# Two graph layers on one core: raw f32 rows gathered from x and h instead of tables of split f16 rows

## The chip, the cores and the metric

The kernel runs on 1 core of a Trainium2 chip. The metric is the device time of the whole program in microseconds. All inputs and outputs lie in HBM. The engines are TensorE (PE), VectorE (DVE), ScalarE (ACT), GpSimd (POOL) and the sequencer SyncE (SP).

## The reference

6250 nodes with 512 numbers each, 106250 edges. Edges come sorted by dst; src and dst are symmetric with one loop for each node.

```python
edge_index = jnp.stack([src, dst])
# layer 0, messages go from src to dst
x_l = x @ W_l.T + b_l
agg = segment_sum(x_l[src], dst, 6250); deg = segment_sum(ones, dst, 6250)
x = layernorm(x + agg / max(deg, 1) + x @ W_r.T)
# layer 1, h = x, messages go from dst to src
msg = h[dst] @ W_neigh.T + b_neigh
neigh = segment_sum(msg, src, n) / max(deg, 1)
y = h + relu(h @ W_self.T + b_self + neigh)
y = layernorm(y) * ln_gamma + ln_beta
out = layernorm(x + y)
```

## The kernel before, in words

Both layers first add up the raw rows of the neighbours and project the mean afterwards. The nodes stand in T = 49 tiles of 128. A layer's edges are put in a list of 928 chunks of 128 edges; two chunks (a group) belong to one tile of target nodes. For each chunk POOL gathers 128 rows with one indirect DMA (L359), VectorE makes a one-hot 128 x 128 that says which target row each edge has (L564), and TensorE multiplies one-hot by rows into one of two pairs of PSUM banks (`sums`, L764). VectorE adds a finished group to the accumulator `acc` of its tile in SBUF (`add`, L577), whose number it loads into a register. The 513th column counts the edges. The semaphore `s_mm` counts finished chunks; `add`, POOL (which reuses a row buffer) and the rings wait for it.

**Tables.** TensorE multiplies f16 in one pass. So each f32 row is stored as two f16 halves, `high` and `low`, scaled by a power of two, with the scale and its inverse in the last 4 f16 places: a table row has 1028 f16, 2056 bytes. For layer 0 the kernel loads all of x into `acc`, takes maxima (L425), and ScalarE, VectorE and POOL make the table (L837, L449, L324 to L327), which SP stores (L264) before the sort begins. For layer 1 the halves are made at the end of each tile of layer 0 (L678, L679) and stored beside `h_scratch` (L286, L288).

**Lists.** Layer 0's list is made from windows of 256 edges: loads L249 to L252, arithmetic L405 to L417, f32 matmuls (L717 to L722), copies L435 to L440. Layer 1's needs a sort by src tile: `prepare(1)` counts (L471) and finds places (L495 to L498, 49 rounds) on VectorE alone. Then each of EC = 832 columns of 128 edges is placed by a matmul of `put` (value at its row) with `where` (one-hot of the chunk, 128 x 928 in two halves). The value has two parts for f16, so there are 4 matmuls a column (`place`, L740). ScalarE makes `put1` and `put2` (L851, L852) from VectorE's `spot` (L590); VectorE makes `where` (L592). The columns are mixed into the first 832 chunks of layer 0's aggregation, one column before each chunk. The result is unpacked after layer 0's last chunk.

**Rings.** `rows` has GB = 8 buffers, `onehot` SB = 8, `put` and `where` PB = 4. The indices of 8 chunks at a time are copied by VectorE (`hand_over`, L554, L555) into a ring of 16.

**Projection.** For each tile ScalarE scales the sums to means (L865), TensorE transposes mean and own row (L805, L808), ScalarE copies them (L873, L874), TensorE does 8 f32 matmuls (L818), VectorE adds, normalizes and writes `res`, SP stores it. In layer 0 POOL clears the tile of `acc` for layer 1 (L340).

The two matmuls of a chunk, its count, and the four of a column (`mm` stands on L703, so all of TensorE's matmuls have that line; its transposes have L805 and L808):

```python
mm(ps[:, bank, :], lhs, row[:, 0:D], start=start, stop=False)
mm(ps[:, bank, :], lhs, row[:, D:2 * D], start=False, stop=stop)
mm(ps[:, bank + 1, 0:1], lhs, row[:, 2 * D + 2:2 * D + 4].bitcast(bf16)[:, 0:1],
   start=start, stop=stop).then_inc(s_mm, 1)
```

Of the kernel before, what the change touches and what calls it, by code (L numbers as in the profile page):

```python
# [15 lines left out]
P = 128  # L16


def gnn_two_layers(nc, x, src, dst, w_l_t, b_l, w_r_t, w_self_t, b_self, w_neigh_t, b_neigh, gamma, beta, out):
# [9 lines left out]
    U = 16  # L29
    H = U // 2  # L30
# [4 lines left out]
    GROUP = (2, 2)  # L35
    GROUPS = [-(-(-(-E // (P * g)) + T - 1) * g // U) * U // g for g in GROUP]

    assert all((E + T * (P * g - 1)) // (P * g) <= n for n, g in zip(GROUPS, GROUP))
    CHUNKS = [n * g for n, g in zip(GROUPS, GROUP)]

    WIN = P * GROUP[0]
# [4 lines left out]
    assert WB * WP == NWIN and GROUPS[0] <= 512 and NWIN + T - 1 <= GROUPS[0]  # L46
    CW = max(CHUNKS)
    EPS = 1e-5
    GB = 8
    SB = 8  # L50
    PB = 4
    TW = 2 * D + 4
    XS = 14
    HS = 10
    assert D ** 0.5 * 2 ** HS < 65504
    BATCH = 7
    NOWHERE = 8191
    assert NOWHERE // P >= T
    assert T % BATCH == 0 and BATCH <= GB

    ctx = ExitStack()
    with ctx:
# [3 lines left out]
        def sem(name):  # L66
            return ctx.enter_context(nc.semaphore(name))


# [4 lines left out]
        iota_chunk = sb("iota_chunk", [P, CW], f16)  # L74
        iota_bin = sb("iota_bin", [P, T], f32)
        eps = sb("eps", [P, 1], f32)
        zeros = sb("zeros", [P, D + 1], f32)

        edges = sb("edges", [P, 2, EC], i32)
        flat = sb("flat", [P, 6 * EC], f32)  # L80
        inta, intb = (flat[:, k * EC:(k + 1) * EC].bitcast(i32) for k in (0, 1))
        val1, val2, run, pos = (flat[:, k * EC:(k + 1) * EC] for k in (2, 3, 4, 5))
# [5 lines left out]
        binf = sb("binf", [P, EC], f16)  # L88
        mask = sb("mask", [P, EC], f16)
# [16 lines left out]
        spot = sb("spot", [P, PB, P], f16)  # L106
        put1 = sb("put1", [P, PB, P], f16)
        put2 = sb("put2", [P, PB, P], f16)
        where = sb("where", [P, PB, CW], f16)
        w_hot = where[0:WP, :, :].bitcast(f32).rearrange("p a c -> p (a c)")[:, 0:WB * GROUPS[0]].rearrange(  # L110
            "p (b c) -> p b c", b=WB)
        past = where[0:T, :, :].bitcast(f32).rearrange("p a c -> p (a c)")[:, 0:CW]

        g_idx = [sb(f"g_idx{l}", [P, CHUNKS[l]], i32) for l in range(2)]
        g_loc = [sb(f"g_loc{l}", [P, CHUNKS[l]], f32) for l in range(2)]
        g_tile = [sb(f"g_tile{l}", [1, CHUNKS[0]], i32) for l in range(2)]
        dst_next = g_idx[1][:, 0:EC]
        idx_ring = sb("idx_ring", [P, U], i32)
        loc_ring = sb("loc_ring", [P, U], f32)
# [7 lines left out]
        top = sb("top", [P, T], f32)  # L127
        scale = sb("scale", [P, T], f32)
        inv = sb("inv", [P, T], f32)

        w_a = sb("w_a", [P, KC, D], f32)
        w_b = sb("w_b", [P, KC, D], f32)

        vec = [where[:, :, :].bitcast(f32).rearrange("p a c -> p (a c)")[:, k * D:(k + 1) * D] for k in range(3)]
        vec += [edges[:, :, :].bitcast(f32).rearrange("p a c -> p (a c)")[:, k * D:(k + 1) * D] for k in range(2)]
        OB = 4
        plain = rows[:, :, :].rearrange("p b w -> p (b w)")
        own = plain[:, 0:2 * OB * D].bitcast(f32).rearrange("p (b d) -> p b d", b=OB)
        res = plain[:, 2 * OB * D:2 * (OB + 2) * D].bitcast(f32).rearrange("p (b d) -> p b d", b=2)
        assert 2 * (OB + 2) * D <= 6 * TW  # L140
        res_tab = rows[:, 6:8, :]
# [10 lines left out]
        tables = [nc.dram_tensor(f"table{l}", [T * P, TW], f16, kind="Internal").ap() for l in range(2)]  # L152
        h_dram = nc.dram_tensor("h_scratch", [T * P, D], f32, kind="Internal").ap()

# [4 lines left out]
        s_x = [sem(f"s_x{k}") for k in range(5)]  # L159
# [5 lines left out]
        s_scale = sem("s_scale")  # L165
        s_high = sem("s_high")
        s_low = sem("s_low")
        s_tail = sem("s_tail")
        s_tab = [sem(f"s_tab{k}") for k in range(BATCH)]
        s_zero = sem("s_zero")  # L170
        s_wn = sem("s_wn")
# [6 lines left out]
        for l in range(2):  # L178
            for name in ("tot", "cnt", "cs", "cscol", "cscp", "past", "tile", "spot", "where", "put", "placed", "list"):
                lists[l][name] = sem(f"s_{name}{l}")  # L180
        s_idx = sem("s_idx")
        s_ring = sem("s_ring")
        s_row = [sem(f"s_row{k}") for k in range(GB)]
        s_hot = sem("s_hot")
# [10 lines left out]
        s_hi = sem("s_hi")  # L195
        s_tails = sem("s_tails")
# [4 lines left out]
        XG = 12  # L201

        def chunk0(layer):

            return layer * CHUNKS[0]

        def group0(layer):
            return layer * GROUPS[0]

        def slot_tiles(slots, k):  # L210

            return (T - 1 - k) // slots + 1

        def stored(layer, t, k):

            n = (t - k) // 2 + 1
            return 32 * n if layer == 0 else 32 * slot_tiles(2, k) + 16 * n
# [15 lines left out]
        def mod2(t, k):  # L233
            return k % 2

        @block.sync
        def _(sp):
            sp.wait_ge(s_pad, 3)
# [26 lines left out]
            for layer in range(2):  # L265
# [16 lines left out]
                def tile(t, k, load_next=True):  # L282
# [4 lines left out]
                    if layer == 0:  # L287
                        sp.dma_start(rows_of(tables[1]), res_tab[0:n, k % 2, :]).then_inc(s_st[k % 2], 16)  # L288
# [624 lines left out]
```

## Time and profile before

| | |
|---|---|
| median of 3 runs | 4260.94 us (4256.3 to 4261.07) |
| span of the profiled execution | 4265.6 us |
| PE busy | 2781.9 us (65%) |
| PE weight loads | 1195.8 us (28%) |
| DVE busy | 2610.8 us (61%) |
| ACT busy | 815.1 us (19%) |
| POOL busy | 1897.4 us (44%) |
| DMA | 586.38 MB, mean 137 GB/s |

The shares are averages over stages that differ much. Times of matmuls in the profile are modelled, and one f32 matmul of the program stands as two records. A line "idle before" tells how long an engine stood still before an instruction and what seems to have released it.

### The profile page before, as it was taken

To read this page: it belongs to the slowest core of one execution; us is meant where nothing else is said; L and a number is where in the kernel's file an instruction comes from. 1 tells how busy PE (TensorE), PEld (TensorE's weight loads), DVE (VectorE), ACT (ScalarE), POOL (GpSimd) and SP (SyncE) were. 2 spreads that over 40 slices of the span, in tenths; PEclk is the share of its full clock that TensorE was granted. 3 is DMA by queue.
4 is the path that set the end of the run, shared out by engine and by line. 5 is a ranking of instruction groups with operands and counts; after the bars stand their busy time and mean duration, and the time that the engine had idled before them with its cause. 6 is when DMAs were issued, how large, how long until landed. Compare 5 with 4: busy or idle time off the path is not lost.

```text
span 4265.6 us, 57125 instructions
## 1 busy us (share of the span) xinstructions
PE 2781.9 (65%) x11308; PEld 1195.8 (28%) x11308; DVE 2610.8 (61%) x6523; ACT 815.1 (19%) x2156; POOL 1897.4 (44%) x2073
## 2 busy tenths in 40 slices
PE   1000188888888888866999655555555555568887
PEld 0000033333333333322455211112111111124443
DVE  3878877777777777754555444444444444448887
ACT  0300044444444444410222000000000000002222
POOL 0600166666666666664000366666666666630000
PEclk9555599999999999977999765665566665669999
DMA  3300066656656666664333566666666666671111
GB/s 140 121 0 0 25 166 166 167 162 165 166 164 164 166 167 166 165 203 136 98 103 103 156 175 178 173 175 173 175 176 176 175 174 170 168 115 59 59 59 49
DMA packets 201222, 586.38 MB, mean 137 GB/s; under 512 B 34672, under 2 KB 35502, under 8 KB 201196
## 3 DMA queue, kind: packets, MB, share of 16 engines
q0 software_dynamic: 148480, 488.56, 42.3%
q1 hardware_dynamic: 52716, 97.53, 7.3%
q8 instruction: 10, 0.16, 0.0%
q14 instruction: 16, 0.13, 0.0%
HBM read 534.51 MB, written 51.44 MB: 137 GB/s over the span
## 4 chain that ended last, share of the span: by engine, by line
PE 39%; DVE 19%; issue 16%; DMA 10%; DVEq 6%; another core or an unknown queue 4%; ACT 2%; SPq 2%; POOL 2%; POOLq 0%; ACTq 0%
PE ps L703 37%; DMA rows<-table,idx_ring 8%; DVE acc L577 4%; DVEq L571 3%; DVE flat L496 2%; DVE onehot L564 2%; POOL rows L359 2%; DVE flat L497 1%; DVE flat L498 1%; DVE where L592 1%; PE ps L805 1%; DVE st L651 1%; PE ps L808 1%; DVE spot L590 1%
## 5 line engine op out<-in xcount | busy, mean ns | idle before, releaser
L359 POOL DMA_INDIRECT rows<-table,idx_ring x1856 | 1794.6, 967 | 1438.0 <-issue 453.5
L703 PE MATMUL ps<-rows,onehot 128*128 128x512 f16 (+1 forms) x5568 | 1378.6, 384 | 782.5 <-DVE acc L577 614.7
L577 DVE TENSOR_TENSOR acc<-acc,ps 128x513 f32 x928 | 638.7, 688 | 850.8 <-remote 328.4
L703 PE MATMUL ps<-where,put 128*128 128x464 f16 x3328 | 801.1, 363 | 380.3 <-ACT put L852 297.8
L703 PEld LDWEIGHTS ps<-rows,onehot 128*128 128x128 bf16 x5568 | 537.3, 113 | 1645.9 <-DVE acc L577 749.2
L564 DVE TENSOR_SCALAR onehot<-iota_node,loc_ring,rows 128x128 bf16<-128x128 f16 x1856 | 583.4, 322 | 281.2 <-DMA rows<-table,idx_ring 250.1
L851 ACT ACTIVATE put<-spot,flat 128x128 f16<-128x128 f16 x832 | 334.1, 402 | 1099.4 <-DVE spot L590 754.3
L703 PEld LDWEIGHTS ps<-where,put 128*128 128x128 f16 x3328 | 267.4, 97 | 696.5 <-issue 371.3
L592 DVE TENSOR_SCALAR where<-iota_chunk,hi_ring 128x928 f16<-128x928 f16 x832 | 380.4, 457 | 0.0
L865 ACT ACTIVATE flat<-acc,rdeg 128x512 f32 (+1 forms) x98 | 69.4, 710 | 1577.5 <-DVE rdeg L640 1574.0
L703 PE MATMUL ps<-w_a,flat 128*128 128x512 f32 x784 | 355.1, 596 | 0.1
L703 PE MATMUL ps<-w_b,flat 128*128 128x512 f32 x784 | 352.4, 592 | 0.0
L852 ACT ACTIVATE put<-spot,flat 128x128 f16<-128x128 f16 x832 | 321.1, 386 | 7.5 <-issue 7.5
L590 DVE TENSOR_SCALAR spot<-iota_node,lo_ring 128x128 f16<-128x128 f16 x832 | 213.3, 256 | 73.8 <-PE ps L703 60.5
L703 PEld LDWEIGHTS ps<-w_b,flat 128*128 128x128 f32 x784 | 149.0, 190 | 187.5 <-issue 187.5
L340 POOL COPY acc<-zeros 128x513 f32 (+1 forms) x49 | 34.4, 702 | 343.2 <-ACT flat L865 343.2
L703 PEld LDWEIGHTS ps<-w_a,flat 128*128 128x128 f32 x784 | 142.5, 192 | 143.4 <-issue 142.5
L884 ACT ACTIVATE sd<-mv,eps 128x1 f32<-128x1 f32 x147 | 43.3, 295 | 626.0 <-DVE mv L656 626.0
L672 DVE SCALAR_TENSOR_TENSOR flat<-where,has,ps 128x512 f32<-128x512 f32 x49 | 36.6, 747 | 133.0 <-PE ps L703 133.0
L703 PE MATMUL ps<-totals,ones 128*128 128x49 f32 x2 | 0.7, 430 | 163.8 <-DVE flat L475 163.8
L651 DVE BATCH_NORM_STATS2 st<-flat 128x6 f32<-128x512 f32 x147 | 102.1, 695 | 5.0
L805 PE MATMUL ps<-ident,flat 128*128 128x128 f32 x392 | 62.3, 283 | 58.8 <-ACT flat L874 48.8
(131 smaller groups left out, 1368.0 us busy)
## 6 DMA issues: line engine op xcount, KB each, us to landing
rows<-table,idx_ring POOLq DMA_INDIRECT x1856
table<-rows SPq DMA_DIRECT2D x98, 257.0 KB, 3.7
h_scratch<-rows SPq DMA_DIRECT2D x49, 256.0 KB, 2.0
rows<-h_scratch SPq DMA_DIRECT2D x49, 256.0 KB, 2.7
acc<-in_x SPq DMA_DIRECT2D x4, 3072.0 KB, 23.5
rows<-in_x SPq DMA_DIRECT2D x48, 256.0 KB, 3.3
out<-rows SPq DMA_DIRECT2D x48, 256.0 KB, 2.0
w_a<-in_w_l_t SPq DMA_DIRECT2D x1, 1024.0 KB
```

What stands on the lines that cost most here:

```text
L359: nc.gpsimd.indirect_dma_start(out=rows[:, k % GB, :], out_offset=None, in_=tables[layer][:, :], in_offset=bass.IndirectOffsetOnAxis(ap=id ...
L496: link(V.tensor_tensor_scan(run, mask[:], mask[:], base[:, ds(b, 1)], ALU.add, ALU.bypass))
L564: V.tensor_scalar(onehot[:, k % SB, :], iota_node[:], loc_ring[:, k:k + 1], rows[:, k % GB, 2 * D:2 * D + 2].bitcast(f32), ALU.is_equal, A ...
L571: tile = dve.value_load(g_tile[layer][0:1, ds(U // g * i + q, 1)], min_val=0, max_val=T - 1)
L577: V.tensor_tensor(tile_acc, tile_acc, part, ALU.add).then_inc(s_acc, 1)
L590: V.tensor_scalar(spot[:, k % PB, :], iota_node[:], lo_ring[:, k:k + 1], None, ALU.is_equal).then_inc(s["spot"], 1)
L592: V.tensor_scalar(where[:, k % PB, 0:CHUNKS[1]], iota_chunk[:, 0:CHUNKS[1]], hi_ring[:, k:k + 1], None, ALU.is_equal).then_inc(s["where"], 1)
L651: V.bn_stats(st[:], dest).then_inc(v, 1)
L703: return nc.tensor.matmul(*args, skip_group_check=True, **kw)
L805: nc.tensor.transpose(ps[:, 0, j * P:(j + 1) * P], mean_nb[:, k % 2, j * P:(j + 1) * P], ident[:])
L851: nc.scalar.activation(put1[:, k, :], spot[:, k, :], ACT.Copy, scale=val1[:, ds(col, 1)])
L852: nc.scalar.activation(put2[:, k, :], spot[:, k, :], ACT.Copy, scale=val2[:, ds(col, 1)]).then_inc(s["put"], 1)
```

## The change

x and h are gathered as they are: 512 f32, 2048 bytes a row. The tables, the load of x into `acc`, maxima, scales, `high`, `low` and all of L678 and L679 are gone. The row matmul is one f32 matmul, the count a second f32 matmul with a column of ones. The one-hots are f32 and are made by ScalarE, 4 chunks at a time: |iota - local row| in bf16 (`apart`), then max(0, 1 - that). ScalarE also hands over the indices. `rows` has 16 buffers, the ring of indices 32. PSUM keeps its two pairs of banks. The placing value is one f32 number, `put` and `where` are f32 and made by VectorE, there are 2 f32 matmuls a column, and PB is 2. Edge loads go out on ScalarE's queue, windows on SP's, each cut so that no large part has 127 or 103 partitions. `acc` is cleared by POOL at the start. ScalarE and POOL may begin with layer 0's chunks when its list is made, before `prepare(1)`.

```diff
-    PB = 4
-    GB = 8
+    PB = 2
+    GB = 16
-        rows = sb("rows", [P, GB, TW], f16)
-        onehot = sb("onehot", [P, SB, P], bf16)
+        rows = sb("rows", [P, GB, D], f32)
+        apart = sb("apart", [P, SB, P], bf16)
+        onehot = sb("onehot", [P, SB, P], f32)
...
+        table = (x, h_dram)
...
@@ sync
-            for k in range(4):
-                sp.dma_start(acc[:, k * XG:(k + 1) * XG, 0:D],
-                             x[k * XG * P:(k + 1) * XG * P, :].rearrange("(t p) d -> p t d", p=P)).then_inc(s_x[k], 16)
...
-                    sp.dma_start(tables[0][ds((BATCH * i + k) * P, P), :], rows[:, k, :]).then_inc(s_tab[k], 16)
...
-                    if layer == 0:
-                        sp.dma_start(rows_of(tables[1]), res_tab[0:n, k % 2, :]).then_inc(s_st[k % 2], 16)
...
@@ gpsimd
             for k in range(7):
-                pool.wait_ge(s_low, (k + 1) * T // 7)
                 nc.gpsimd.memset(acc[:, k * T // 7:(k + 1) * T // 7, :], 0.0).then_inc(s_zero, 1)
...
-                            out=rows[:, k % GB, :], out_offset=None, in_=tables[layer][:, :],
+                            out=rows[:, k % GB, :], out_offset=None, in_=table[layer][:, :],
...
@@ vector
-                V.tensor_scalar(spot[:, k % PB, :], iota_node[:], lo_ring[:, k:k + 1], None,
-                                ALU.is_equal).then_inc(s["spot"], 1)
-                V.tensor_scalar(where[:, k % PB, 0:CHUNKS[1]], iota_chunk[:, 0:CHUNKS[1]], hi_ring[:, k:k + 1], None,
+                V.tensor_scalar(put[:, k % PB, :], iota_node[:], lo_ring[:, k:k + 1], val_ring[:, k:k + 1],
+                                ALU.is_equal, ALU.mult)
+                V.tensor_scalar(where[:, k % PB, :], iota_chunk[:], hi_ring[:, k:k + 1], None,
                                 ALU.is_equal).then_inc(s["where"], 1)
...
@@ tensor, place and sums
-                for n, put in enumerate((put1, put2)):
-                    for b in range(2):
-                        last = mm(ps[:, 2 * n + b, 0:half], put[:, k % PB, :],
-                                  where[:, k % PB, b * half:(b + 1) * half], start=start, stop=stop)
+                for b in range(2):
+                    last = mm(ps[:, b, 0:HALF], put[:, k % PB, :], where[:, k % PB, b * HALF:(b + 1) * HALF],
+                              start=start, stop=stop)
...
+                    if k % (H // 2) == 0:
+                        pe.wait_ge(s_hot, 2 * (layer * BATCHES + U // H * i) + k // (H // 2) + 1)
+                    if k % G == 0 and not (first and q < 2):
+                        pe.wait_ge(s_acc, layer * GROUPS + U // G * i + q - 1)
+                    pe.wait_ge(s_row[k], 16 * (layer * ROUNDS + i + 1))
+                    mm(ps[:, bank, :], lhs, rows[:, k, :], start=start, stop=stop)
+                    mm(ps[:, bank + 1, 0:1], lhs, ones[:, 0:1], start=start, stop=stop).then_inc(s_mm, 1)
...
@@ scalar
+            def hand_over(layer, j, slot, first=False):
+
+                if not first:
+                    act.wait_ge(s_mm, layer * CHUNKS + H * (j - R + 1))
+                nc.scalar.activation(idx_ring[:, H * slot:H * (slot + 1)], g_idx[layer][:, ds(H * j, H)],
+                                     ACT.Copy).then_inc(s_idx, 1)
+
+            def hots(layer, j, first=False):
+                half = H // 2
+                for b in range(2):
...
+                    for k in range(half):
+                        last = nc.scalar.activation(apart[:, half * b + k, :], iota_node[:], ACT.Abs,
+                                                    bias=g_neg[layer][:, ds(H * j + half * b + k, 1)])
+                    last.then_inc(s_apart, 1)
+                for b in range(2):
+                    act.wait_ge(s_apart, 2 * (layer * BATCHES + j) + b + 1)
...
+                        act.wait_ge(s_mm, layer * CHUNKS + H * (j - 1) + half * (b + 1))
+                    nc.scalar.activation(onehot[:, half * b:half * (b + 1), :], apart[:, half * b:half * (b + 1), :],
+                                         ACT.Relu, bias=ones[:, 0:1], scale=-1.0).then_inc(s_hot, 1)
```

## Rows read from the trace of the kernel before

**Rows 1.** Busy time by stretch: us, PE, PEld, DVE, ACT, POOL, clock, DMA share, GB/s

```profile
162.00:518.00 356.00, 3.11 (x10) 1.49 (x10) 303.37 (x325) 0.11 (x1) 21.27 (x8) 0.50 0.01 2
518.00:1848.00 1330.00, 1116.05 (x5825) 507.61 (x5826) 976.40 (x3222) 578.26 (x1664) 830.42 (x837) 0.98 0.61 165
1848.00:1991.00 143.00, 78.22 (x288) 27.23 (x287) 60.13 (x164) 0.00 (x0) 86.78 (x92) 0.65 0.68 196
1991.00:2378.00 387.00, 378.95 (x1170) 190.19 (x1171) 217.07 (x396) 94.26 (x196) 34.42 (x49) 0.98 0.33 97
...
2391.00:3720.00 1329.00, 743.05 (x2638) 255.27 (x2639) 573.45 (x1539) 0.00 (x0) 833.28 (x882) 0.62 0.63 176
3720.00:3805.00 85.00, 46.18 (x149) 14.56 (x145) 33.26 (x80) 0.00 (x0) 44.13 (x47) 0.52 0.95 146
3805.00:4266.00 461.00, 392.57 (x1178) 187.82 (x1176) 361.99 (x690) 107.71 (x245) 0.00 (x0) 0.97 0.17 56
```

**Rows 2.** Chain of waits from 944 to 954 us: start, us, what

```profile
946.12 6.35 PE ps L703 x35
```

**Rows 3.** Timeline of POOL in layer 1: start, us, instruction, idle before

```profile
2819.48 0.94 POOL L359 DMA_INDIRECT rows<-table,idx_ring  x1 [0.30 <-issue]
2820.73 0.95 POOL L359 DMA_INDIRECT rows<-table,idx_ring  x1 [0.30 <-issue]
```

**Rows 4.** Who TensorE waited for, 2400 to 3700 us: us, times, longest

```profile
PE ps L703 <- DVE acc L577: 450.4, 235, 6.2
```

**Rows 5.** Timeline of layer 1, 2783 to 2794 us

```profile
2786.35 1.07 PE L703 MATMUL ps<-rows,onehot 128*128 128x512 f16 x6 [1.80 <-DVE acc L577]
...
2791.40 0.69 DVE L577 TENSOR_TENSOR acc<-acc,ps 128x513 f32 x1 [4.21 <-remote]
```

**Rows 6.** Timeline of SP's queue at the start

```profile
12.09 16.56 SPq L241 DMA_DIRECT2D edges<-in_dst  x1
```

**Rows 7.** Timeline, 158 to 192 us

```profile
162.00 21.28 POOL L331 MEMSET acc<- 128x3591 f32 x7
162.46 21.26 DVE L462 TENSOR_SCALAR flat<-edges 128x832 int32<-128x832 int32 x1 [0.80 <-issue]
```

**Rows 8.** Timeline of the first 140 us

```profile
3.29 0.28 POOL L317 TENSOR_SCALAR_AFFINE_SELECT ident<-ident 128x128 f32<-128x128 f32 x1
...
70.53 1.29 DVE L405 CAST flat<-flat 104x1024 f32<-104x1024 int32 x2 [10.36 <-DMA flat<-in_dst]
...
80.10 18.54 PE L703 MATMUL ps<-where,flat 104*128 104x464 f32 x40 [5.99 <-DVE where L417]
...
111.00 0.58 DVE L435 TENSOR_TENSOR flat<-ps,iota_chunk 128x464 f32<-128x464 f32 x1
```

**Rows 9.** Groups by line and shape: count, busy us, mean ns, idle before

```profile
L577 DVE TENSOR_TENSOR acc<-acc,ps 128x513 f32 x928 | 638.7, 688 | 850.8 <-remote 328.4 <-PE ps L703 308.0 <-issue 210.7
...
L703 PE MATMUL ps<-w_a,flat 128*128 128x512 f32 x784 | 355.1, 596 | 0.1
...
L851 ACT ACTIVATE put<-spot,flat 128x128 f16<-128x128 f16 x832 | 334.1, 402 | 1099.4 <-DVE spot L590 754.3 <-issue 183.7 <-PE ps L703 129.0
...
L865 ACT ACTIVATE flat<-acc,rdeg 128x512 f32 x80 | 56.8, 710 | 3.5 <-issue 3.5
...
L415 DVE TENSOR_SCALAR flat<-ones,w_d 104x128 f32<-104x128 f32 x4 | 1.1, 281 | 0.0
...
L491 DVE TENSOR_SCALAR where<-iota_chunk,cs_col 49x928 f32<-49x928 f16 x1 | 0.7, 697 | 0.0
```

**Rows 10.** Timeline, 72 to 91 us; the last row is from 70 to 73 alone

```profile
72.93 1.18 PE L703 MATMUL ps<-w_n,ones 104*104 104x3 f32 x6
...
90.31 0.19 PEld L703 LDWEIGHTS ps<-where,flat 104*128 104x128 f32 x1 [0.20 <-issue]
90.70 0.19 PEld L703 LDWEIGHTS ps<-where,flat 104*128 104x128 f32 x1 [0.20 <-issue]
...
72.93 0.31 PE L703 MATMUL ps<-w_n,ones 104*104 104x3 f32 x1
```

More of the change, by code:

```diff
@@ L29, in gnn_two_layers @@
     U = 16
-    H = U // 2
+    H = 8
+    R = 4
+    UP = H * R
     EC = -(-(-(-E // P)) // U) * U
     EFULL, EREST = E // EC, E - E // EC * EC
[L35 to L41, printed above, removed]
+    G = 2
+    GROUPS = -(-(-(-E // (P * G)) + T - 1) * G // UP) * UP // G
+    CHUNKS = GROUPS * G
+    HALF = CHUNKS // 2
+    ROUNDS = CHUNKS // U
+    BATCHES = CHUNKS // H
+    assert (E + T * (P * G - 1)) // (P * G) <= GROUPS and HALF <= 512
+    WIN = P * G
     NWIN = -(-E // WIN)
@@ L126, in gnn_two_layers @@
         has = sb("has", [P, T], f32)
[L127 to L135, printed above, removed]
-        OB = 4
[L137 to L141, printed above, removed]
+        OB = 4
+        own = rows[:, 0:OB, :]
+        res = rows[:, OB:OB + 2, :]
         mean_nb = flat[:, 0:2 * D].rearrange("p (b d) -> p b d", b=2)
@@ L164, in gnn_two_layers @@
         v = sem("v")
[L165 to L169, printed above, removed]
         s_zero = sem("s_zero")
+        s_clear = sem("s_clear")
         s_wn = sem("s_wn")
@@ L178, in gnn_two_layers @@
         for l in range(2):
-            for name in ("tot", "cnt", "cs", "cscol", "cscp", "past", "tile", "spot", "where", "put", "placed", "list"):
+            for name in ("tot", "cnt", "cs", "cscol", "cscp", "past", "tile", "where", "placed", "list"):
                 lists[l][name] = sem(f"s_{name}{l}")
+        s_listed = sem("s_listed")
         s_idx = sem("s_idx")
@@ L252, in _, with tile_of, load, tile @@
                 sp.dma_start(win_i[a][WP - 1:WP, WB - 1, 0:WREST],
                              given[(NWIN - 1) * WIN:E].rearrange("(p j) -> p j", p=1)).then_inc(s_wins, 16)
[L254 to L264 removed]
+            def tile_of(layer):
+                target = (h_dram, out)[layer]
+                source = table[layer]
+                def load(t, k, n=P):
+                    sp.dma_start(own[0:n, k, :], source[ds(t * P, n), :] if not isinstance(t, int)
+                                 else source[t * P:t * P + n, :]).then_inc(s_own[k], 16)
+                def tile(t, k):
+                    n = LAST if layer == 1 and isinstance(t, int) and t == T - 1 else P
+                    sp.wait_ge(s_res, layer * T + t + 1)
+                    rows_of = (lambda a: a[t * P:t * P + n, :]) if isinstance(t, int) else (lambda a: a[ds(t * P, n), :])
+                    sp.dma_start(rows_of(target), res[0:n, k % 2, :]).then_inc(s_st[k % 2], 16)
+                    if not isinstance(t, int) or t + OB < T:
+                        last = isinstance(t, int) and t + OB == T - 1
+                        load(t + OB, k, LAST if last and layer == 0 else P)
+                return load, tile
@@ L642, in _ @@
                     dve.wait_ge(s_vec, 16 * 5)
[L643 to L647 removed]
+                begun, per = steps[0], (4, 11)[layer]
                 def norm_stats(dest, n):
@@ L731, in prepare @@
                 pe.wait_ge(s["past"], 1)
-                half = GROUPS[layer] // 2
+                half = GROUPS // 2
                 for b in range(2):
@@ new lines, in _, with round_of @@
+            for layer in range(2):
+                act.wait_ge(s_listed, layer + 1)
+                if layer:
+                    act.wait_ge(s_zero, 7 + T)
+                for j in range(2):
+                    hand_over(layer, j, j, first=(layer == 0))
+                def round_of(i, first=False, last=False):
+                    for b in range(R):
+                        j = R * i + b
+                        if not (last and b >= R - 2):
+                            hand_over(layer, j + 2, (b + 2) % R, first=(first and b < 2))
+                        hots(layer, j, first=(first and b == 0))
+                round_of(0, first=(layer == 0))
+                with act.Fori(1, BATCHES // R - 1) as i:
+                    round_of(i)
+                round_of(BATCHES // R - 1, last=True)
```

390 lines of the change are left out of this document (136 added, 254 removed).

## The prediction

> **What bounds the kernel now.** I first cut the span into its stages with the table of busy time by stretch [rows 1]. No engine bounds them all. From 162 to 518 us VectorE is alone (303 of 356 us): it sorts the edges of layer 1 into tiles (count, place). From 518 to 1848 us TensorE is busy for 1116 of 1330 us at a granted clock of 0.98: this is layer 0's aggregation with the 832 placing columns of layer 1's list mixed in. The chain of waits there runs through TensorE in unbroken pieces such as 35 matmuls in 6.35 us [rows 2], five columns of 1.27 us each; with its stalls a column takes 1330 / 832 = 1.60 us. From 1991 to 2378 and from 3805 to 4266 are the dense projections, where TensorE is again dense. Between them lies layer 1's aggregation, 2391 to 3805, and nothing in it is full: TensorE 56%, VectorE 43%, POOL 63%, DMA 0.63. Its 882 gathers of the first 1329 us come every 1.51 us, though POOL by itself issues one every 1.25 us (0.95 busy and 0.30 of issue) [rows 3]. So a round trip sets it: TensorE waited 450 us for VectorE's adds [rows 4]. One such wait is shown in [rows 5]: matmuls begin at 2786.35 and last 1.07 us, but the next add, of this group or of the one before it, starts at 2791.40, after VectorE had been idle for 4.21 us. TensorE's "done" signal comes late there, and with two PSUM groups and eight row buffers TensorE and POOL both run dry. The clock, 0.62, is a mix of the two levels (1.2 and 2.4 GHz). In the last 85 us the gathers fetch one and the same padding row and the DMA engines are full (0.95) [rows 1].
>
> **The change, part by part.** I sum against the profiled execution's own span, 4265.6 us. It is 4.7 us above the median of the timed runs, 4260.94, and I take these 4.7 us off at the end.
>
> *Before the aggregation.* Gone are the load of x into acc, the maxima, the table of scaled halves and its 49 stores: all that lies between the window lists and 162 us. Now the edges go out on ScalarE's queue and the windows on SP's, and the 127-partition loads, of which one holds SP's queue for 16.56 us [rows 6], are cut into 112 and 15. What then sets the start is a lock: POOL's clearing of acc took 21.28 us, and VectorE's L462, one shift of 832 numbers, took 21.26 us beside it [rows 7]. That clearing now begins at about 3 us, so VectorE may not get going before about 25. From there: 9.6 us of window arithmetic (70.53 to 80.10), 18.5 us of list matmuls (they stay f32), seven list copies of 0.58 us, 4 us [rows 8]: 57 us. If the lock spares the small operations, the loads decide and it is 47; if the edge loads come in late, 70. Then the sort, from 183.7 to 518 us before, without the locked instruction: 334 us. Aggregation begins at 57 + 334 = 391, against 518: a gain of 127 us.
>
> *A placing column.* Before: four f16 matmuls of 464 columns and two of 512 for the rows. Now the two halves of the value are one f32 number: two f32 matmuls of 464. But f32 isn't one pass. The list matmuls, 20 in the code, stand as 40 records, and the projections as 784 for 392 [rows 8, 9]; at full clock the records of 464 columns follow each other every 0.387 us (weight loads at 90.31 and 90.70) [rows 10]. So placing costs 2 x 2 x 0.387 = 1.55 us where 4 x 464 / 2.4 GHz = 0.77 us stood. The row matmul costs 2 x 0.427 = 0.85 us (0.387 x 512 / 464) instead of 0.43. The column of ones is two more records, whose weight loads nothing covers: six such pairs of 104 columns took 1.18 us with a last latency of 0.31, so 0.174 us each, two cycles a column at 1.2 GHz [rows 10]; for 128 columns at the higher one that is 0.107, and 0.21 for two. A column: 1.55 + 0.85 + 0.21 = 2.61 us. Weight loads beside long matmuls cost nothing here, because the spacing of 0.387 us is already 464 columns twice at 2.4 GHz. The Trainium skill (TensorE: Matmul & The Clock Gate, The mechanism) says that weight loads overlap running matmuls only when they go to other row groups. By that, the six loads of a column that I count as hidden would show with 0.107 us each, 3.25 us in all; the spacing in the trace disagrees.
>
> Does something else take longer than 2.61 us? VectorE: an f32 place matrix of 928 costs 0.70 us (L491, 49 partitions, is nearest), the put 0.28 (L415), half an add 0.34, ring copies 0.03, about 0.1 of sequencing: 1.45 us. ScalarE: 8 distances of 0.40 (L851), two ramps of at most 0.71 and a copy of 0.2 for 8 chunks: 0.6 us each [rows 9]. POOL: 1.25. All are covered by TensorE; uncovered (layer 1's pace of 1.25) they still lie below it, VectorE without placing. With only two place buffers VectorE must answer within 3.5 us (row matmul, placing, row matmul) and needs 1.0 for the matrix, 1.7 with an add ahead; a signal late by 2 us just fits, one like [rows 5] doesn't. I add 0.03 for these: 2.64 (bounds 2.61, and 2.9 if one column in seven waits 2 us). 832 x 2.64 = 2196 us against 1330: a loss of 866 us.
>
> *The last 96 chunks of layer 0, and layer 1.* A chunk costs TensorE 0.85 + 0.21 = 1.07 us at full clock, POOL 1.25. Sixteen row buffers instead of eight and ScalarE's one-hots take row landings and VectorE's queue out of the loop, so POOL can run on. What stays is the pair of PSUM groups: the next group but one waits for "done", VectorE's wake-up and add (0.69), about 0.9 us, of the 2.1 us that a group takes, so a signal may be 1.2 us late; [rows 5] shows 4. One stall of 2.3 us in ten chunks gives 1.07 + 0.23 = 1.30. Lower bound 1.25 (POOL), upper 1.50 (as now); I take 1.35, nearer to POOL's row, for the ring is doubled and a queue refills TensorE after a stall. Layer 0: 96 x 1.35 = 130 against 143, 13 gained. Layer 1: 882 x 1.35 = 1191 against 1329, 138 gained. The 85 us of padding stay: DMA sets them, and the bytes are the same but for 8 in 2056.
>
> *Projections.* TensorE's 8 f32 matmuls and 8 transposes a tile set layer 0's (379 of 387 us busy); the two dropped VectorE operations lay beside them. Between the layers the last store no longer waits for them: 2 us.
>
> Sum: 4265.6 - 127 + 866 - 13 - 138 - 2 = 4852; less 4.7: **4847 us**, 14% slower.
>
> **The rivals.**
> 1. *Layer 1 gains nothing*, because the late signals and not the ring set 1.50: 96 + 882 gathers at 0.15 more, +147: **4994**. For it: [rows 4, 5]. Against: POOL's gaps now come from eight buffers.
> 2. *Two place buffers are too few*: 2.9 us a column, +216: **5063**. For it: TensorE's signals are late in placing too (1.60 against 1.27 us a column). Against: the slack of 3.5 us.
> 3. *The clock falls in layer 1*: a chunk of 2.13 us instead of 1.35, +690: **5537**. For it: 0.62 with 56% busy. Against: at that level TensorE would have no gaps, and every stretch with 80% busy or more shows 0.97 or 0.98 [rows 1]. The Trainium skill (TensorE: Matmul & The Clock Gate, HAM oscillation) says idle gaps between bursts bring the clock down; that would be this case.
> 4. *Weight loads show*: six more loads a column, 0.64 us, +533; layer 1's chunk (two more, 1.28) stays under 1.35: **5380**. Against: [rows 10].
> 5. *Not slower*: f32 matmuls of 0/1 matrices and values run as one pass. A column would be 0.77 + 0.43 + 0.11 = 1.31 for TensorE and VectorE's 1.45 would set it: 990 us less, **3857**. It decides from 1.94 us a column downwards (2.64 less 586 / 832). Against: two records for each f32 matmul, whatever the data, the ones matrix included.
>
> **How the numbers follow.** Chances: forecast 0.6, rival 1 0.17, rival 2 0.12, rival 3 0.03, rival 4 0.02, rival 5 0.04, others 0.02. The forecast's own range is 4715 (layer 1 and layer 0's end at POOL's 1.25, lists at 47 us, column 2.61) to 4950; with rivals 1 and 2 the range is 4700 to 5060. Runs of this kernel agree within 0.1%, so 0.2% is what a measurement can tell. Faster 0.05, same 0.01, slower 0.94.
>
> **What the profile will show.** Placing: TensorE over 95% busy at clock 1, 48 matmul records (six columns) in about 16 us, and a stretch of 2.2 ms. Start of the first gather near 60 us, of the first row matmul near 391. Layer 1: gathers 1.25 to 1.4 us apart, clock above 0.85. Wrong I am if a column takes under 2.5 or over 2.8 us, if the clock of layer 1 stays near 0.6, or if TensorE still waits hundreds of us there for adds.

## The result and the profile after

The changed kernel takes 5015.85 us (median of 4 runs, 5013.79 to 5024.8) against 4260.99 for the kernel before (4 runs beside it, 4256.3 to 4261.07): 1.178 times the time, 95% interval 1.176 to 1.179. Forecast was 4847, with a range to 5060 and rival 1 at 4994. The profiled execution spans 5013.9 us, 748.3 more than before.

The table of busy time by stretch of the changed kernel, cut where its stages change (us, then PE, PEld, DVE, ACT, POOL busy, the granted clock, DMA share, GB/s), answers to [rows 1]:

```profile
56.00:391.00 335.00, 3.11 (x10) 1.49 (x10) 281.22 (x321) 7.68 (x23) 15.71 (x16) 0.50 0.04 13
391.00:2588.00 2197.00, 2196.24 (x6653) 1135.06 (x6654) 1095.74 (x2231) 400.25 (x1134) 787.52 (x831) 1.00 0.35 99
2588.00:2726.00 138.00, 113.28 (x386) 62.45 (x385) 33.12 (x48) 43.18 (x120) 76.78 (x81) 0.94 0.60 181
2726.00:3118.00 392.00, 383.53 (x1180) 191.78 (x1178) 151.09 (x299) 94.34 (x196) 32.03 (x50) 0.99 0.19 65
3118.00:4470.00 1352.00, 1082.48 (x3485) 591.94 (x3486) 301.95 (x440) 426.52 (x1212) 837.83 (x884) 0.90 0.60 173
4470.00:4555.00 85.00, 71.04 (x228) 38.65 (x227) 20.49 (x32) 23.80 (x65) 41.69 (x44) 0.88 0.72 142
4555.00:5014.00 459.00, 393.18 (x1176) 188.18 (x1176) 360.81 (x687) 107.77 (x245) 0.00 (x0) 0.97 0.17 56
```

Read it from the top. The sort ends at 391, 127 us earlier than before. Then TensorE is busy for 2196.24 of 2197 us at full clock. From the first placing matmul (391.76) to the end of the last (2587.82) it takes 2196 us, or 2.64 us a column: 867 us more than the 1329 that the same measure gives before. That is as forecast. The last 96 chunks of layer 0 end at 2726.43, after 139 us (143 before, 130 forecast). The fifth line is the one that is off: the gathers of layer 1 take 1352 us, 1.53 us each, where 1.35 were forecast and 1.51 were measured before. TensorE has 270 us without work there, and its granted clock is 0.90.

The view of waits of the changed kernel in that stretch (us, times, longest) tells what TensorE waits for; the row that answers to [rows 4] is the last:

```profile
DVE acc L468 <- PE ps L576: 598.3, 218, 13.2
...
ACT onehot L728 <- PE ps L576: 483.7, 129, 12.7
DVE acc L468 <- remote: 251.9, 46, 13.3
PE ps L576 <- DVE acc L468: 234.0, 105, 10.0
```

One such stop in its timeline, the like of [rows 5]:

```profile
3288.76 1.10 PE L576 MATMUL ps<-rows,onehot 128*128 128x512 f32 x2
...
3289.70 0.28 PE L576 MATMUL ps<-ones,onehot 128*128 128x1 f32 x2
...
3290.30 0.95 POOL L306 DMA_INDIRECT rows<-h_scratch,idx_ring  x1 [0.30 <-issue]
...
3290.92 1.10 PE L576 MATMUL ps<-rows,onehot 128*128 128x512 f32 x2
...
3291.86 0.28 PE L576 MATMUL ps<-ones,onehot 128*128 128x1 f32 x2
...
3293.17 0.69 DVE L468 TENSOR_TENSOR acc<-acc,ps 128x513 f32 x1 [4.52 <-PE ps L576]
3293.18 0.72 ACT L728 ACTIVATE onehot<-apart,ones 128x512 f32<-128x512 bf16 x1 [2.17 <-PE ps L576]
3293.80 0.95 POOL L306 DMA_INDIRECT rows<-h_scratch,idx_ring  x1 [2.55 <-PE ps L576]
3293.91 0.30 PEld L576 LDWEIGHTS ps<-rows,onehot 128*128 128x128 f32 x2 [1.86 <-DVE acc L468]
```

A group of two chunks is complete at 3289.98 (3289.70 + 0.28) and the next at 3292.14. VectorE adds the first only at 3293.17, 3.2 us later. In the same instant ScalarE, which waits for a later count of the same signal, begins its one-hots, and POOL's next gather follows 0.6 us later. So TensorE's "done" signals come late and in one batch.

The packed trace also records when increments of `s_mm` took effect. Chunks that ended at 3288.90, 3289.98 and 3291.06 were counted at 3293.04, 3293.10 and 3293.16, so the first of them 4.1 us late. Of layer 1's 928 increments 769 are recorded, and 437 of these came more than 0.1 us after TensorE's latest matmul had ended; the semaphores that VectorE and ScalarE increment were never late. In the placing, with a gather every 2.64 us, none of the 831 recorded was more than 0.02 us late. For the kernel before, the same record has 512 of 692 late in the placing and 381 of 689 in layer 1.

### The profile page after: what moved, and what is told of

Its sections match the earlier page's. It is cut to its first block, busy times and chain, and to the rows that moved or that the text cites. A ratio compares the mean times of both kernels' runs of the same rounds, so it can differ in the third digit from the quotient of the medians.

```text
span 5013.9 us, 56364 instructions
## 1 busy us (share of the span) xinstructions
PE 4262.5 (85%) x13164; PEld 2219.8 (44%) x13164; DVE 2274.0 (45%) x4093; ACT 1103.6 (22%) x2995; POOL 1815.2 (36%) x1926
## 4 chain that ended last, share of the span: by engine, by line
PE 77%; DVE 11%; another core or an unknown queue 5%; issue 5%; DVEq 2%; ACT 1%; DMA 0%; SPq 0%; ACTq 0%; POOLq 0%
PE ps L576 75%; DVE flat L410 2%; DVE acc L468 2%; DVE flat L412 1%; DVE flat L411 1%; DVEq L462 1%; PE ps L669 1%; DVE st L525 1%; PE ps L672 1%; DVE stage L409 0%; DVE flat L555 0%; DVE flat L560 0%; DVE flat L557 0%; DVE flat L562 0%
## 5 line engine op out<-in xcount | busy, mean ns | idle before, releaser
L576 PE MATMUL ps<-rows,onehot 128*128 128x512 f32 x3712 | 2090.0, 651 | 308.1 <-DVE acc L468 267.2
L576 PE MATMUL ps<-stage 128*128 128x464 f32 x3328 | 1501.7, 574 | 250.1 <-DVE stage L483 250.1
L306 POOL DMA_INDIRECT rows<-in_x,idx_ring x928 | 880.0, 948 | 1808.8 <-PE ps L576 1737.6
L576 PEld LDWEIGHTS ps<-ones,onehot 128*128 128x128 f32 x3712 | 742.6, 200 | 959.1 <-issue 959.1
L306 POOL DMA_INDIRECT rows<-h_scratch,idx_ring x928 | 879.5, 948 | 558.3 <-PE ps L576 227.8
L576 PEld LDWEIGHTS ps<-rows,onehot 128*128 128x128 f32 x3712 | 656.7, 200 | 653.4 <-issue 418.9
L576 PEld LDWEIGHTS ps<-stage 128*128 128x128 f32 x3328 | 569.3, 191 | 582.5 <-issue 582.5
L483 DVE TENSOR_SCALAR stage<-iota_chunk,hi_ring 128x928 f32<-128x928 f16 x832 | 580.3, 697 | 0.0
L721 ACT ACTIVATE apart<-iota_node,g_neg 128x128 bf16<-128x128 f16 x1856 | 564.1, 386 | 0.0
L576 PE MATMUL ps<-ones,onehot 128*128 128x1 f32 x3712 | 533.4, 213 | 0.0
```

The lines of the kernel that those rows point to most:

```text
L306: nc.gpsimd.indirect_dma_start(out=rows[:, k % GB, :], out_offset=None, in_=table[layer][:, :], in_offset=bass.IndirectOffsetOnAxis(ap=idx ...
L483: V.tensor_scalar(where[:, k % PB, :], iota_chunk[:], hi_ring[:, k:k + 1], None, ALU.is_equal).then_inc(s["where"], 1)
L576: return nc.tensor.matmul(*args, skip_group_check=True, **kw)
L721: last = nc.scalar.activation(apart[:, half * b + k, :], iota_node[:], ACT.Abs, bias=g_neg[layer][:, ds(H * j + half * b + k, 1)])
```

## The experiments

The twelve runs below fell on four chips, and each was run beside the kernel before. That time turned out to matter more than most edits: in eleven of the runs, on three chips, the kernel before took 3784 to 3788 us and not 4261. I call a chip of the first kind prompt and one of the second kind late. Each chip was used at one time only, so a lasting trait of a chip and a passing state of it are not told apart. The times of experiments 1 to 3 are single executions.

**1. Layer 1 taken apart.** Four edits of the changed kernel. The first has four PSUM pairs instead of two in layer 1 (VectorE's `add` reads the same pair):

```
+def pair(layer, q):
+    return 2 * (q % 4) if layer else 4 + 2 * (q % 2)
...
-bank = 4 + 2 * (q % 2)
+bank = pair(layer, q)
...
-pe.wait_ge(s_acc, layer * GROUPS + U // G * i + q - 1)
+pe.wait_ge(s_acc, layer * GROUPS + U // G * i + q - (1, 3)[layer])
```

> The changed kernel with four PSUM pairs instead of two in layer 1's aggregation, nothing else. Theory A (TensorE's late done signals run out the slack of two PSUM pairs): a chunk of layer 1 falls from 1.53 us to 1.25 to 1.30, that is 200 to 245 us less than 5016, about 4790, and TensorE's wait for adds in that stretch (234 us) nearly goes. Theory B (POOL's issue and the ring of rows set the pace): within 20 us of 5016. Theory C (ScalarE's one-hots, eight buffers, set it): within 60 us of 5016, and the wait for adds turns into a wait for one-hots.

The second adds eight more one-hot buffers in layer 1 (`hot_b`, in `flat`) and lets ScalarE run two batches ahead of TensorE.

> Four PSUM pairs and sixteen one-hot buffers instead of eight in layer 1. Theory A alone: the same as four pairs alone, about 4790 (POOL's 1.25 us a chunk is the floor: 4770). Theory C, or A with the one-hots next in line: at least 30 us below four pairs alone. Theory B: within 20 us of 5016.

The third leaves the gathers of layer 1 out, and TensorE's wait for them:

```
-nc.gpsimd.indirect_dma_start(
+if layer == 0: nc.gpsimd.indirect_dma_start(
...
-pe.wait_ge(s_row[k], 16 * (layer * ROUNDS + i + 1))
+if layer == 0:
+    pe.wait_ge(s_row[k], 16 * (i + 1))
```

> Layer 1 issues no gathers at all and TensorE does not wait for rows (its sums are made from what lies in the row buffers; the gathers of layer 1 are left out). If TensorE's done signals are late because of the gathers (POOL's issuing or their traffic), a chunk of layer 1 falls to TensorE's own 1.07 to 1.10 us: 884 x 0.45 = 400 us less and 35 us less in the padding, about 4580. If the signals are late by themselves, the chunk stays near 1.5 us and only the padding's 15 us go: about 5000.

The fourth gathers 64 numbers where a row has 512. It reads h as rows of 64, so its rows also lie in the first eighth of h:

```
+given = (x, h_dram.rearrange("r (a c) -> (r a) c", c=64))
...
-out=rows[:, k % GB, :], out_offset=None, in_=table[layer][:, :],
+out=rows[:, k % GB, 0:(D, 64)[layer]], out_offset=None, in_=given[layer][:, :],
```

> Layer 1 issues all its gathers, but each row is 64 numbers instead of 512 (7/8 of each gathered row of layer 1 is left out). If the bytes make the signals late or set the pace: a chunk at POOL's 1.25 us, 250 us less, and 25 us less in the padding, about 4740. If POOL's issuing (its descriptors, the same number as before) does it: within 40 us of 5016.

Measured: 4739.76, 4740.57, 4558.74 and 4737.95 us, beside a kernel before of 3787.71. Three of four agree within 3 us whatever they change, so they can't be read against 5016; the unedited pair had to be run on such a chip.

**2. Both kernels again, with controls.**

> The changed kernel itself, unedited, as a control beside the other three. In the first four runs the kernel before took 3788 us instead of 4261, so lateness of TensorE's signals may belong to the chip and not to the kernel. If this run's kernel before is again near 3788 and theory D (the late signals belong to a chip or its state) holds: about 4740, layer 1 at POOL's 1.25 us a chunk. If the kernel before is near 4261: 5016 with 1.53 us a chunk. If four PSUM pairs had done it (theory A): 5016 whatever the kernel before takes.

> The kernel before, unedited, for its profile. Theory D: where it takes 3788 us its 473 us are gone in the stretches with gathers alone, layer 0's aggregation (1330 us; 832 columns of 1.27 are 1057, 270 less) and layer 1 (1.51 us a gather falling to POOL's 1.25: 230 less), and its prologue and projections last as before.

> Four PSUM pairs in layer 1, again. Beside a kernel before of 3788: equal to the control within 10 us (theory D). Beside a kernel before of 4261: theory A says 4790 against the control's 5016, since four pairs have 2.1 us more slack for each pair of groups than two; if the signals come only when TensorE stops, the four pairs gain half or less (over 4890).

Measured beside a kernel before of 3783.55: the changed kernel 4739.36, the kernel before 3784.96, four PSUM pairs 4737.32. On a prompt chip the changed kernel takes 4739.36 / 3783.55 = 1.253 times as long, 956 us more. Four pairs, sixteen one-hots and the bytes of a row make no difference there (3 us at most). The kernel before on a prompt chip, by stretch: the placing, the last 96 chunks, layer 1's gathers.

```profile
516.00:1611.00 1095.00, 1052.16 (x5823) 507.76 (x5824) 979.81 (x3221) 576.47 (x1664) 835.71 (x836) 1.00 0.73 201
1611.00:1735.00 124.00, 83.15 (x291) 27.50 (x289) 63.15 (x165) 0.00 (x0) 87.08 (x92) 0.62 0.77 226
2136.00:3239.00 1103.00, 752.24 (x2630) 249.87 (x2631) 596.87 (x1533) 0.00 (x0) 834.52 (x881) 0.63 0.74 211
```

And the changed kernel on the same chip, the same three:

```profile
391.00:2588.00 2197.00, 2196.36 (x6654) 1135.09 (x6655) 1094.84 (x2231) 400.14 (x1134) 786.68 (x831) 1.00 0.35 99
2588.00:2695.00 107.00, 105.50 (x388) 58.86 (x386) 33.11 (x48) 43.20 (x120) 76.74 (x81) 1.00 0.77 233
3092.00:4195.00 1103.00, 1023.67 (x3512) 571.24 (x3513) 302.22 (x439) 426.52 (x1210) 834.47 (x882) 1.00 0.71 211
```

The placing of the changed kernel takes 2196 us on both kinds of chip; on the late one, too, no signal is late in it. The kernel before takes 1094 us here (1.31 us a column, first placing matmul to last) and 1329 on the late chip. Layer 1's 881 gathers take 1103 us in both kernels, 1.252 us each, with TensorE busy 752 us in one and 1024 in the other: POOL sets it. All 928 increments of `s_mm` in layer 1 are recorded in both traces, and none is more than 0.02 us late.

What a late chip adds is, for the kernel before, 234 + 20 + 225 = 479 us (placing, last 96, layer 1), and for the changed kernel 0 + 31 + 241 = 272 (its layer 1 goes from the first gather at 3122.79 to the 882nd at 4466.39, 1344 us); the spans differ by 482 and 276.

With no gathers at all (run 3 of the first four) TensorE sets layer 1:

```profile
3092.00:4030.00 938.00, 937.97 (x3462) 523.61 (x3463) 298.18 (x432) 420.63 (x1193) 0.00 (x0) 1.00 0.01 2
```

TensorE is full for 938 us, 3462 records or 866 chunks of four: 1.08 us a chunk, the 1.07 of the forecast. VectorE and ScalarE keep up. With an eighth of the bytes POOL still issues a gather every 1.25 us, 0.94 busy and 0.30 between:

```profile
3500.08 0.94 POOL L308 DMA_INDIRECT rows<-h_scratch,idx_ring  x1 [0.30 <-issue]
3501.33 0.94 POOL L308 DMA_INDIRECT rows<-h_scratch,idx_ring  x1 [0.30 <-issue]
```

**3. The f32 placing undone.** The changed kernel with the value in two f16 parts, four place buffers and four f16 matmuls of 464:

```
-    PB = 2
+    PB = 4
...
-last = mm(ps[:, b, 0:HALF], put[:, k % PB, :], where[:, k % PB, b * HALF:(b + 1) * HALF], ...)
+for n in range(2):
+    last = mm(ps[:, 2 * n + b, 0:HALF], put[:, n, k % PB, :], where[...], ...)
```

> The changed kernel with the placing of the kernel before (value in two parts, four f16 matmuls of 464, four place buffers) on VectorE; rows stay f32. TensorE's column: 0.77 + 0.85 + 0.21 = 1.84 us instead of 2.65, so 832 x 0.81 = 674 us below the control beside it (about 4066 where the control is 4740, 4342 or somewhat more where it is 5016). If the f32 rows and not the f32 placing make the column dear: less than 400 us below.

Measured: 4025.66 us beside the same kernel before (3783.55) and the control (4739.36): 714 us less. Its placing stretch:

```profile
391.00:1874.00 1483.00, 1481.28 (x6653) 829.64 (x6654) 999.41 (x3120) 400.20 (x1134) 808.59 (x830) 1.00 0.52 147
```

The placing goes from 392.72 to 1874.04: 1481 / 832 = 1.78 us a column instead of 2.64. So the f32 placing costs 0.86 us a column (0.81 expected), 0.86 x 832 = 715 us and thus the whole difference, and the f32 rows cost the other 0.47 over the 1.31 of the kernel before. TensorE is still the bound, busy for 1481 of 1483 us. So the f32 rows alone cost 1481 - 1094 = 387 us in the placing. Against that stand 124 us gained at the start, 17 in the last 96 chunks and 4 between the layers, and this version is 242 us slower than the kernel before.

**4. What is left at either end of the changed kernel.** ScalarE clears acc; four PSUM pairs; POOL waits for TensorE before every fourth gather.

```
-for k in range(7):
-    nc.gpsimd.memset(acc[:, k * T // 7:(k + 1) * T // 7, :], 0.0).then_inc(s_zero, 1)
+def wipe(t, k):   # on ScalarE
+    nc.scalar.activation(acc[:, ds(t, 1), :], zeros, ACT.Copy).then_inc(s_zero, 1)
-if not (first and k < GB):
-    used = n - GB + 1
+if k % 4 == 0 and not (first and k < GB):
+    used = n - GB + 4
```

> The changed kernel with three edits in stages of their own: ScalarE instead of POOL clears acc at the start; four PSUM pairs in layer 1; POOL waits for TensorE before every fourth gather instead of each. Where the kernel before takes about 3785 us (signals prompt, the changed kernel 4739): VectorE's shift at 10.5 us takes 0.2 us and not 13.9, so the aggregation starts at 377 instead of 391; POOL's bound in layer 1 falls from 1.25 us to 0.95 + 0.30 / 4 = 1.03, TensorE's 1.07 sets the pace: 882 x 0.17 = 150 us less. Together about 4575. If 1.25 were not POOL's but another loop's: 4725. Where the kernel before takes about 4261 (signals late, 5016): theory A, four pairs take the late signals' cost, gives at most 1.30 us a chunk, 4800 or less; if the signals come only when TensorE stops, 1.45 or more, over 4930.

Measured: 4731.21 beside 3788.1, only 8 below the control (on another prompt chip). The changed kernel has a lock like that of [rows 7] at its start, as the timeline of the control shows:

```profile
3.08 21.27 POOL L279 MEMSET acc<- 128x3591 f32 x7
10.53 13.86 DVE L342 TENSOR_SCALAR w_ti<-flat 104x4 int32<-104x4 int32 x1 [6.27 <-DMA flat<-in_src]
```

Here it is gone: ScalarE's 49 copies lie beside VectorE's shift.

```profile
9.28 25.61 ACT L714 ACTIVATE acc<-onehot 128x513 f32<-128x513 f32 x49
9.79 0.17 DVE L345 TENSOR_SCALAR w_ti<-flat 104x4 int32<-104x4 int32 x1 [5.54 <-DMA flat<-in_src]
```

It takes 0.17 us, the first gather starts at 43.8 instead of 58.5, and the placing starts 13 us earlier. Some 4 us of it are lost again in the last 96 chunks of layer 0 and 2 to 3 in the padding; why, I did not find out. But my theory of the 0.30 us was wrong: layer 1 still takes 1101 us. POOL's timeline there, three gathers of four without a wait:

```profile
3500.40 0.95 POOL L309 DMA_INDIRECT rows<-h_scratch,idx_ring  x1 [0.30 <-issue]
3501.65 0.95 POOL L309 DMA_INDIRECT rows<-h_scratch,idx_ring  x1 [0.30 <-issue]
3502.90 0.94 POOL L309 DMA_INDIRECT rows<-h_scratch,idx_ring  x1 [0.30 <-PE ps L580]
```

The 0.30 us stands between gathers with and without a wait. It belongs to the gather, and 1.25 us is POOL's whole price for one.

**5. The same on the kernel before**, to beat both: ScalarE clears acc and four PSUM pairs; then also a wait before every second gather only (the edits are those shown; ScalarE clears each tile of acc once its table rows are made, and the wait has k % 2).

> The kernel before with two edits: ScalarE instead of POOL clears acc after the tables; four PSUM pairs instead of two in layer 1. The shift L462 takes 0.6 us instead of 21.5, so the sort ends 21 us earlier. Where the kernel before takes about 3785: 3764 (four pairs change nothing, POOL's 1.25 us is the bound). If ScalarE's clearing slows VectorE too: 3785. Where it takes about 4261: 4240 less what four pairs give, up to 230 (1.51 to 1.25 us a gather).

> The same two edits on the kernel before, and POOL waits before every second gather. Where the kernel before takes about 3785: layer 1's gathers every 0.97 + 0.30 / 2 = 1.12 us instead of 1.25, 882 x 0.13 = 115 us less, and in the last 96 chunks of layer 0 some 10 less: about 3640. If another loop (eight row buffers: a row takes 2.8 us to land) is next in line at once: 3740 to 3764. Where it takes about 4261: the same as without this edit, or worse, since a ring of eight that is given back in pairs has one buffer less of slack.

Measured: 3767.09 us, 0.9948 of the kernel before (interval 0.9931 to 0.9964), and 3771.84, 0.9957 (0.994 to 0.9974), both beside 3788.1. The first is what one shift gives, 0.59 us instead of the 21.26 of [rows 7]; layer 1 stays at 1102 us. It is the fastest version found on a prompt chip, by 0.5%, and faster than both kernels there. The second shows that fewer waits give nothing; 5 us are lost in the placing (1097 against 1091 us), perhaps because the buffers come back in pairs, which no run shows.

**6. Four PSUM pairs on a late chip.** The f16 placing, ScalarE's clearing and the four pairs together.

> The changed kernel (raw f32 rows, no tables) with the placing of the kernel before (two f16 parts), ScalarE clearing acc, and four PSUM pairs in layer 1. Where the kernel before takes about 3787 (signals prompt): the f16 placing alone gave 4026, the start comes 13 us earlier, four pairs give nothing: 4012, still 6% slower than the kernel before. Where the kernel before takes about 4261 (signals late): a column of 1.76 to 1.9 us, and layer 1 tells what four PSUM pairs do there: theory A 1.25 to 1.30 us a chunk against 1.53 with two pairs (total about 4050 to 4150, faster than the kernel before); if the signals come only when TensorE stops, 1.45 or more (over 4200).

This run fell on a late chip: 4267.62 us (10 runs, 4264.12 to 4275.77) beside 4271.94 (13 runs), ratio 0.9995, interval 0.9984 to 1.0005: no difference from the kernel before. Its placing and its layer 1:

```profile
382.00:1860.00 1478.00, 1478.00 (x6648) 827.49 (x6647) 996.64 (x3104) 400.19 (x1134) 811.83 (x830) 1.00 0.52 147
2400.00:3727.00 1327.00, 1066.70 (x3481) 585.03 (x3481) 299.52 (x434) 416.90 (x1200) 832.87 (x881) 0.88 0.59 175
```

The column is as good as on the prompt chip, 1.78 us from 380.06 to 1860.31, with 18 of 817 recorded increments of `s_mm` over 0.1 us late. Layer 1 takes 1327 / 881 = 1.51 us a chunk with four pairs; with two pairs it took 1.53, on a chip where the kernel before needed 11 us less. Theory A (late signals run out the slack of two pairs) expected 1.25 to 1.30, and falls. The stops are fewer and longer, as the view of waits of this kernel between 2500 and 3700 us says:

```profile
PE ps L588 <- DVE acc L478: 158.9, 31, 8.8
...
PE ps L588 <- ACT onehot L748: 62.1, 23, 4.9
```

These are 31 stops of 5.1 us for adds and 23 of 2.7 for one-hots in 1200 us, where two pairs had 105 of 2.2 in 1352. One in its timeline:

```profile
3021.44 1.10 PE L588 MATMUL ps<-rows,onehot 128*128 128x512 f32 x2
...
3022.38 0.28 PE L588 MATMUL ps<-ones,onehot 128*128 128x1 f32 x2
...
3022.90 0.94 POOL L310 DMA_INDIRECT rows<-h_scratch,idx_ring  x1 [0.30 <-issue]
3026.59 0.69 DVE L478 TENSOR_TENSOR acc<-acc,ps 128x513 f32 x1 [8.72 <-remote]
3026.61 1.33 ACT L748 ACTIVATE onehot<-apart,ones 128x512 f32<-128x512 bf16 x2 [6.38 <-remote]
3027.12 0.94 POOL L310 DMA_INDIRECT rows<-h_scratch,idx_ring  x1 [3.28 <-remote]
...
3027.57 2.04 PE L588 MATMUL ps<-rows,onehot 128*128 128x512 f32 x2 [4.91 <-ACT onehot L748]
```

VectorE is without work for 8.72 us while TensorE goes on to 3022.66. Then TensorE and POOL both stand still, and only 3.9 us later the waiters are released, VectorE and ScalarE at once and POOL 0.5 us after them. The record of `s_mm` has no increment between 3017.05 and 3026.35 and then eight within 0.5 us; the first of them counts a chunk that ended at 3015.09. With more slack TensorE runs on longer, and a signal comes later: from the end of a group's last matmul to the start of its add pass 3.8 us in the median over layer 1 with four pairs, 1.4 with two, and 0.15 on a prompt chip, where it is never above 0.23.

## Why the prediction was right, and where it was not

The forecast was 14% slower, its range went to 19%, and 18% was measured. The sign and the large term are right for the reason given. Layer 1's gain was not there, and the time lies nearest to rival 1. One of the prediction's own signs of being wrong was met: TensorE still waits 234 us for adds in layer 1.

*Start at 391.* The placing starts at 391.8 and the first row matmul at 395.0, as forecast; POOL's clearing did lock VectorE at the start, and the experiment without it had the first gather 14.7 us earlier.

*A column 2.64 us.* It took 2.64, and the chain of waits from 1500 to 1550 us is one piece of TensorE:

```profile
1499.66 50.52 PE ps L576 x153
```

The doubling of every f32 matmul (4 records of 464 columns for two matmuls) is thereby right, rival 5 is false, and so is rival 4: nothing of 0.64 us a column was added. That the sum is exact is in part luck, as one column in the timeline shows:

```profile
1501.67 1.80 PE L576 MATMUL ps<-stage 128*128 128x464 f32 x4
1503.31 1.02 PE L576 MATMUL ps<-rows,onehot 128*128 128x512 f32 x2
1504.16 0.28 PE L576 MATMUL ps<-ones,onehot 128*128 128x1 f32 x2
1504.31 1.80 PE L576 MATMUL ps<-stage 128*128 128x464 f32 x4
```

From start to start the place matmuls take 1.64 us (1.55 forecast), the row matmul 0.85 (0.85) and the ones 0.15 (0.21), and the 0.03 for stalls is not there. By the Trainium skill (TensorE: Matmul & The Clock Gate, The mechanism), weight loads overlap only matmuls on other row groups. By that rule and 0.107 us for each of six more loads the estimate is 3.25 us a column; the trace has 2.64. Rival 2 is false too, even on the late chip that the prediction was measured on: the placing lasts 2196 us on both kinds. But the reason given against it, a slack of 3.5 us, was not put to the test. In this stretch no signal was late at all.

*Last 96 chunks 130 us, between the layers 2 us less.* They were 139 us and 4 us less.

*Layer 1 at 1.35 us a chunk: the term that failed.* It was 1.52 (1344 us from the first gather to the 882nd, where 1191 were forecast), and this is 153 of the 162 us by which the span's 748 exceed the sum's 586; the last 96 chunks are 9 more, and the rest cancels. The forecast was 1.07 of work and 0.23 of stalls, set up to 1.35. The stalls for adds came nearly as forecast: 105 in 884 chunks, 2.2 us each, 0.26 us a chunk. With 36 us of other gaps TensorE is idle for 0.31 us a chunk. The larger part of the miss is TensorE's own work: it is busy for 1082 us, 1.22 a chunk, where the run without gathers has 1.08 and the control on a prompt chip, with gaps between its chunks, 1.16, both at clock 1.00. The clock, put at nothing outside rival 3, is 0.90 here. An estimate from that row is 270 us at the lower level, where half the work is done, so 135 us or 0.15 us a chunk at most. Whether all of it would have been saved at full clock, no run shows, since TensorE might then have waited longer for the same signals.

I took the ring of eight row buffers for half of the cause because POOL's gaps showed there. No run changes the ring alone on a late chip. From before to after, TensorE's waits for adds fell from 450 to 234 us while its busy time rose from 743 to 1082, so that the equal pace of 1.51 and 1.53 doesn't tell what the ring did. Rival 1 said that layer 1 gains nothing (4994 against 5016), and I gave it 0.17. That the stalls nearly came out is luck: the prediction allowed a signal to be 1.2 us late, read 4 in [rows 5], and took one stall in ten chunks without a reason.

Even rival 1's reason was only half right: it blames late signals running out the slack of two PSUM groups. Experiment 6 doubled that slack, and the pace was 0.02 us a chunk better. The lateness is no fixed delay that buffers can cover; with more of them, on another late chip, it was larger (3.8 against 1.4 us in the median).

*The gain in layer 1 that was forecast* can't exist on a prompt chip at all: there both kernels stand at POOL's 1.25 us and the change gives 0. On such a chip the sum is -125 + 1102 - 16 - 4 + 0 - 2 = 955 us (start, placing, last 96, the stretch between the layers, layer 1, the rest), on the late one -127 + 867 - 5 - 4 + 15 + 2 = 748 (with the padding last). The same change thus costs 18% on a late chip and 25% on a prompt one, because the kernel before loses 479 us more on the late chip and the changed one 272. The forecast of 14% was made from a late chip's profile and would have missed a prompt chip's 25%; the placing alone decides the sign on both.

*Rival 3, the clock.* It was 0.90 in layer 1 and not near 0.6, so the rival is false in its size of 690 us, but a part of it is in the miss above. In experiment 6 TensorE stood still from 3022.66 to 3027.57; then two records take 2.04 us instead of 1.10, and the granted clock from 3027.5 to 3030 is 0.50.

*Still open:* what releases the late signals. In the two stops shown the release comes 1.0 and 3.9 us after TensorE's last matmul ended, and 2.9 and 3.7 us after POOL's last gather started. The changed kernel's layer 1 has 92 batches (two or more increments of `s_mm` less than 0.1 us apart, after more than 2.3 us with none). In the middle 80% of them the first increment comes 2.1 to 2.8 us after the start of the last gather, but 0.5 to 2.6 us after TensorE's last end. On a prompt chip a gather takes 3.6 us (median) from issue to landing:

```profile
rows<-h_scratch,idx_ring POOLq DMA_INDIRECT x865, 3.6
```

So the release keeps a steadier distance to the last gather in flight than to TensorE's own work. That would fit signals held back while gathers are under way. It would also fit that lateness goes with the pace of the gathers: none late in the placing at 2.64 us a gather, 18 of 817 at 1.78, 512 of 692 at 1.60. But it was only read from times: the two runs that would tell (no gathers, and small ones) fell on a prompt chip, as did the sixteen one-hot buffers. Another reading stands untested too. Three kernels with different buffers and different work for TensorE have the same pace in layer 1 on late chips (1.51, 1.53, 1.51 us a gather), as they would if something in the path of the gathers set it and the late signals only followed. Against that, a gather's packets are done no later there: 3.6 us after its start in layer 1 of the changed kernel on both kinds of chip (median of their times in the trace). Nor is it known why chips differ.

## What to carry to other kernels

Before taking a wait for a matter of buffers, compare its longest cases with what the buffers can cover. Here VectorE's longest waits were several times the slack, and with twice the buffers the stops were only rarer and longer. A step that fills an engine completely (the f32 placing) costs its full price, 867 us here. That it lost nothing on a late chip says nothing for full engines, since no signal was late there. And price the stage's floor first: layer 1 could never have come below POOL's 1.25 us a gather, so the most that deeper buffers could give on the late chip was 0.26 us a chunk, against 1.04 us a column paid there for the simpler form. Last, run both kernels on one chip before comparing anything.

## What the runs showed of the hardware that was not expected

- The same kernel takes 3784 to 3788 us on three chips, and 4261 and 4272 us in the two measurements on late ones. The difference is in stretches with gathers under way; the projections and the sort last the same on both (between the layers 400 and 401 us, the end 461 and 460 us).
- On a late chip only TensorE's increments are late: in layer 1 of the changed kernel 437 of 769 recorded come more than 0.1 us after its latest matmul has ended, then in batches 0.06 us apart, and none of VectorE's or ScalarE's. On a prompt chip all 928 come within 0.02 us.
- A gather of 128 rows costs POOL 1.25 us (0.95 busy, 0.30 between) whether or not it waits, and whether a row has 2048 or 256 bytes.
- ScalarE clears acc in 25.6 us (49 copies of 513 numbers) without slowing VectorE, whose shift took 0.17 us beside it; beside POOL's seven memsets of the same tile, 21.3 us in all, shifts of 0.17 and 0.59 us took 13.9 and 21.3 us, until the last memset ended.
